# The first norm's four-element operations on GpSimd, its row sums in halves, and the last five batches scattered tile by tile

## What is computed

```python
xn = layernorm(x)                       # (x - m) / sqrt(v + 1e-5), no weights
q, k, v = relu(xn @ Wq + bq), relu(xn @ Wk + bk), relu(xn @ Wv + bv)
a = softmax(mask(q k^T / 4)) @ v        # 16 heads of 16; causal mask, mask of rows whose sum of xn is 0
attn = gamma * norm(a + xn) + beta      # second norm, eps 1e-8
moe = sum over the 2 best of 8 experts of w * (silu(xn w1) * (xn w3)) w2
out = x + attn + moe + shared expert of xn
```

## Time and profile before

| what | us |
|---|---|
| median of 3 runs | 2209.66 (2207.64 to 2210.34) |
| profiled execution, own time | 2199.74 |
| its span, first to last instruction | 2198.0 |
| attention phase, to the first instruction of the next | 1160.8 |
| expert phase | 1037.2 |

### The profile page before, as it was taken

One profiled execution on the slowest core, in us unless ns is written; L12 is line 12 of the kernel. 1 busy time (PEld: TensorE's weight loads), 2 busy tenths in 40 slices (PEclk: granted clock), 3 DMA queues, 4 the chain that ended last, 5 costly groups with the idle time before them and its releaser, 6 DMA issues. The chain is left out here.

```text
span 2198.0 us, 37336 instructions
## 1 busy us (share of the span) xinstructions
PE 1900.2 (86%) x13238; PEld 1375.1 (63%) x13238; DVE 1401.7 (64%) x2935; ACT 1082.8 (49%) x2048; POOL 1129.4 (51%) x935
## 2 busy tenths in 40 slices
PE   0368988888888888899676999999999999899998
PEld 0245544454554444555325888888888888788887
DVE  6577887788878888876513465656565543355556
ACT  0115555555455555555344666666666665333232
POOL 5444324544554454453423676867777764344443
PEclk9769999999999999999878999999999999999999
DMA  1653655666566666666345566666666654334443
GB/s 36 115 98 81 115 100 120 131 123 129 124 128 136 122 128 125 123 124 129 96 145 168 178 208 203 211 204 199 211 194 216 191 182 153 115 118 141 142 141 110
DMA packets 235391, 314.01 MB, mean 143 GB/s; under 512 B 18986, under 2 KB 200372, under 8 KB 229044
## 3 DMA queue, kind: packets, MB, share of 16 engines
q1 hardware_dynamic: 222964, 278.63, 51.0%
q0 software_dynamic: 12288, 33.57, 4.8%
HBM read 211.43 MB, written 100.70 MB: 142 GB/s over the span
## 5 line engine op out<-in xcount | busy, mean ns | idle before, releaser
L495 ACT ACTIVATE pT<-st_ps 128x512 f32<-128x512 f32 (+1 forms) x704 | 384.1, 559 | 477.0 <-PE st_ps L995 382.1
L1671 PE MATMUL gu<-xc,w_up_h 128*128 128x512 f32 x1760 | 553.1, 396 | 23.6 <-POOL w_up_l L1370 17.1
L719 DVE TENSOR_REDUCE mx<-s_ps 128x1 f32<-128x512 f32 (+3 forms) x704 | 436.2, 638 | 154.3 <-PE s_ps L974 123.4
L972 PE MATMUL s_ps<-k_aug,q_aug 97*128 97x512 bf16 (+3 forms) x1024 | 294.5, 320 | 138.8 <-DVE mx L719 124.0
L1671 PEld LDWEIGHTS gu<-xc,w_up_h 128*128 128x128 f32 x1760 | 326.3, 190 | 103.9 <-issue 18.0
L1671 PE MATMUL gu<-xc,w_up_l 128*128 128x512 f32 x880 | 345.1, 392 | 0.0
L1548 DVE TENSOR_TENSOR hf<-sil,gu 128x512 f32<-128x512 f32 x220 | 151.0, 686 | 258.8 <-ACT sil L1467 258.6
L1370 POOL TENSOR_TENSOR w_up_l<-w_raw,w_up_h 128x512 fp32r<-128x512 f32 x160 | 204.0, 1298 | 210.9 <-ACT w_up_h L1462 210.9
L993 PE MATMUL st_ps<-q_aug,k_aug 99*128 99x512 bf16 (+3 forms) x1024 | 286.5, 313 | 21.8 <-ACT pT L495 14.2
L972 PEld LDWEIGHTS s_ps<-k_aug,q_aug 97*128 97x128 bf16 x1024 | 101.9, 101 | 321.5 <-DVE mx L719 233.3
L411 POOL DMA_INDIRECT expert_rows<-xrow,slot x128 | 125.2, 978 | 314.5 <-DMA q_aug<-neg_scr 249.2
(11 more groups left out here) (207 smaller groups left out, 3418.1 us busy)
## 6 DMA issues: line engine op xcount, KB each, us to landing
w_raw<-in_L_ffn_w_dram SPq DMA_DIRECT2D x117, 512.0 KB, 6.0
part_scr<-parts SPq DMA_DIRECT2D x64, 384.0 KB, 9.3
q_aug<-part_scr SPq DMA_DIRECT2D x192, 128.0 KB
k_aug<-part_scr SPq DMA_DIRECT2D x192, 128.0 KB
xr<-expert_rows SPq DMA_DIRECT2D x39, 512.0 KB
expert_results<-yo SPq DMA_DIRECT2D x39, 512.0 KB, 3.3
x_sb<-in_L_attn_x_dram SPq DMA_DIRECT2D x16, 512.0 KB
layernorm_rows<-xn SPq DMA_DIRECT2D x16, 512.0 KB
```

What stands on the lines that cost most here:

```text
L495: fn(pT[:, j % 2, h:h + heads, 0:w], unit_view(st_ps[u % 2], heads, w), ACT.Exp).then_inc(exp_done, 1)
L719: vec.tensor_reduce(mx[:, q, h:h + heads], unit_view(s_ps[u % 2], heads, keys), AX_X, ALU.max).then_inc(s_max, 2)
L972: mm(v[:, n], q_aug[par][0:ROWS_S, h0 + n, P * q:P * (q + 1)], k_aug[par][0:ROWS_S, h0 + n, 0:keys], start=True, stop=False)
L1671: last = mm(gu[m % 2][:, a], w_up[wpar][x][:, a, c, P * m:P * (m + 1)], xc[par][:, y, c], start=k == 0, stop=k == 3 * NC - 1)
```

## The change

- **DVE keeps** the large operations of the first norm, the reciprocals and the bit cuts. **POOL takes** the folds, the multiplications and the rest of the root: 32 operations a batch beside its power. DVE's two-constant operations become two on POOL, with constants from a new tile `norm_consts`. Where DVE went on by itself, there are now semaphores both ways (`mean_part`, `mean_ready`, `var_part`, `s1_ready`, `r0_ready`, `d1_ready`, `r1_ready`, `root_ready`, `rd_ready`, `mask_part`, `mask_sum`).
- **Row sums** (mean, variance, mask) are made in halves of two tiles, in neighbouring units, so that a maximum comes between them. Some steps move by a unit: centre 3 to 4, product 24 to 25, bits 26 to 27, masks 41 and 42 to 40, 41 and 43.
- **Scatters**: body 14 does batches 11, 12 and 13, body 15 batches 14 and 15, each tile behind every third exponential; the wait for the negated maxima falls away in body 14. Fetches and bounds on SP move to fit.
- **Zeros**: `fill_ends` is done for four experts in body 14, once the table stands, ahead of `load_neg`, and for four in body 15. It no longer waits for the scatters.

```diff
-        AT_NORM = (1, 2, 3, 14, 15, 18, 20, 24, 26, 41, 42)
+        AT_MEAN, AT_CENTRE, AT_VAR = (1, 2), 4, (13, 14)
+        AT_R0, AT_R1, AT_RD, AT_QUOT, AT_BITS = 18, 20, 23, 25, 27
+        AT_MASKS = (40, 41, 43)
...
         def scattered_in(i):
-            if i == B - 1:
-                return list(range(B - GB, B))
-            return [i - 3] if 3 <= i < B - 1 else []
+            if i >= B - 2:
+                return {B - 2: [B - 5, B - 4, B - 3], B - 1: [B - 2, B - 1]}.get(i, [])
+            return [i - 3] if i >= 3 else []
...
-            def fill_ends():
+            def fill_ends(experts):
 
                 await_(sp, table_ready, 1)
-                for k in range(2):
-                    await_(sp, scattered[k], 16 * 2 * NT * (B // 2))
-                for e in range(E):
...
                     store_parts(i + 2, 1)
+                for b in scattered_in(i)[2:]:
+                    fetch(b)
+                if i == B - 2:
+                    fill_ends(range(E // 2))
                 if maxima:
                     load_neg(i + 1, 1 - par, 0)
                 for b in scattered_in(i + 1)[:2]:
                     fetch(b)
-                for b in scattered_in(i)[2:]:
-                    fetch(b)
                 if i == B - 1:
-                    fill_ends()
+                    fill_ends(range(E // 2, E))
 
             iterations(sp, body)
+            for k in range(2):
+                await_(sp, scattered[k], 16 * 2 * NT * (B // 2))
             await_(sp, filled, 16 * E)
...
+            small_begin, small_mark, small_op, small_end = chain(pool, chain_small, 28)
+
+            def fold4(a, b, final):
+                small_op(gp.tensor_tensor(tree2[:], a, b, ALU.add))
+                t2 = tree2[:].rearrange("p t (a b) -> p t a b", b=2)
+                small_op(gp.tensor_tensor(tree3[:], t2[:, :, :, 0], t2[:, :, :, 1], ALU.add))
+                return gp.tensor_tensor(final, tree3[:, :, 0], tree3[:, :, 1], ALU.add)
...
+            def small_mean(b):
+                small_begin(b)
+                await_(pool, mean_part, 2 * (b + 1))
+                small_op(fold16(s[SUM]))
+                await_(pool, a_ready, b)
+                gp.tensor_tensor(s[MEAN], s[SUM], inverse, ALU.mult).then_inc(mean_ready, 1)
+
+            def small_variance(b):
+                await_(pool, var_part, 2 * (b + 1))
+                small_op(fold4(lanes[:, :, 0:4], lanes[:, :, 4:8], s[SUM]))
+                small_op(gp.tensor_tensor(s[T1], s[SUM], inverse, ALU.mult))
+                small_op(gp.tensor_tensor(s[V1], s[T1], eps, ALU.add))
+                gp.tensor_tensor(s[S0], s[V1], half[:], ALU.pow).then_inc(s1_ready, 1)
+
+            def small_step(b):
+
+                await_(pool, r0_ready, b + 1)
+                small_op(gp.tensor_tensor(s[Q1], s[V1], s[R0], ALU.mult))
+                small_op(gp.tensor_tensor(s[T1], s[Q1], s[S0], ALU.add))
+                gp.tensor_tensor(s[D1], s[T1], half[:], ALU.mult).then_inc(d1_ready, 1)
+
+            def small_root(b):
+
+                await_(pool, r1_ready, b + 1)
+                small_mark(gp.tensor_tensor(s[SL], s[D1], s[SH], ALU.subtract))
...
+                small_op(gp.tensor_tensor(s[T1], s[T3], half[:], ALU.mult))
+                gp.tensor_tensor(s[ROOT], s[T1], s[D1], ALU.add).then_inc(root_ready, 1)
+
...
+            def small_parts(b):
+                await_(pool, root_ready, b + 1)
+                await_(pool, rd_ready, b + 1)
+                small_mark(gp.tensor_tensor(s[DL], s[ROOT], s[DH], ALU.subtract))
+                small_op(gp.tensor_tensor(s[NRD], s[RD], minus, ALU.mult))
+
+            def small_mask(b):
+                await_(pool, mask_part, 2 * (b + 1))
+                await_(pool, mk_ready, b)
+                fold16(s[MASK_SUM]).then_inc(mask_sum, 1)
+                small_end()
...
                 mine = scattered_in(i)
                 one = mine[0] if len(mine) == 1 else None
-                for b in mine if one is None else []:
-                    scatter(b, range(NT))
+                if norm:
+                    small_mean(i + 3)
+
+                if one is None:
+                    for n in range(len(mine) * NT):
+                        await_(pool, exp_done, NU * i + 2 + 3 * n)
+                        scatter(mine[n // NT], [n % NT])
 
...
-                    await_(pool, v1_ready, i + 4)
-                    gp.tensor_tensor(sm[:, 2], sm[:, 1], half[:], ALU.pow).then_inc(s1_ready, 1)
+                    small_variance(i + 3)
                 if project:
                     second(i + 2, 2)
+                if norm:
+                    small_step(i + 3)
                 if project:
                     second(i + 2, 3)
                     third(i + 2, 2)
+                if norm:
+                    small_root(i + 3)
                 if one is not None:
                     scatter(one, [2])
                 if project:
                     third(i + 2, 3)
                 if norm:
+                    small_parts(i + 3)
                     quotient(i + 3)
                 if one is not None:
                     scatter(one, [3])
+                if norm:
+                    small_mask(i + 3)
...
+            def row_sums(rows_, h):
+
+                t_ = slice(2 * h, 2 * h + 2)
+                return vec.tensor_reduce(lanes[:, t_], rows_[:, t_].rearrange("p t (k l) -> p t l k", l=16), AX_X,
+                                         ALU.add)
+
+            def ln_mean(b, h):
+                if h == 0:
+                    await_(dve, x_in, 16 * (b + 1))
+                    await_(dve, mask_sum, b)
+                row_sums(x_sb, h).then_inc(mean_part, 1)
 
             def ln_centre(b):
-                ln(vec.tensor_scalar(sm[:, MEAN], sm[:, SUM], 1.0 / C, None, ALU.mult))
+                await_(dve, mean_ready, b + 1)
+                await_(dve, normed, b)
                 for i in range(NT):
                     last = vec.tensor_scalar(ln_a[:, i], x_sb[:, i], sm[:, MEAN, i:i + 1], None, ALU.subtract)
                 last.then_inc(a_ready, 1)
 
-            def ln_var(b):
-
-                await_(dve, sq_done, b + 1)
-                ln(vec.tensor_reduce(lanes[:, :, 0:8], ln_t[:].rearrange("p t (w k) -> p t w k", k=C // 8), AX_X,
-                                     ALU.add))
-
-            def ln_var_fold(b):
-                fold4(lanes[:, :, 0:4], lanes[:, :, 4:8], sm[:, SUM], ln)
-                vec.tensor_scalar(sm[:, V1], sm[:, SUM], 1.0 / C, LN1_EPS, ALU.mult, ALU.add).then_inc(v1_ready, 1)
-
-            s = [sm[:, k] for k in range(20)]
-
-            def ln_root(b):
-
+            def ln_var(b, h):
+                if h == 0:
+                    await_(dve, sq_done, b + 1)
+                t_ = slice(2 * h, 2 * h + 2)
+                vec.tensor_reduce(lanes[:, t_, 0:8], ln_t[:, t_].rearrange("p t (w k) -> p t w k", k=C // 8), AX_X,
+                                  ALU.add).then_inc(var_part, 1)
+
+            def ln_r0(b):
                 await_(dve, s1_ready, b + 1)
-                ln(vec.reciprocal(s[R0], s[S0]))
-                ln(vec.tensor_tensor(s[Q1], s[V1], s[R0], ALU.mult))
-                ln(vec.tensor_tensor(s[T1], s[Q1], s[S0], ALU.add))
-                ln(vec.tensor_scalar(s[D1], s[T1], 0.5, None, ALU.mult))
-                ln_mark(vec.reciprocal(s[R1], s[D1]))
-
-                ln(vec.tensor_scalar(s[SH].bitcast(U32), s[D1].bitcast(U32), HIGH_BITS, None, ALU.bitwise_and))
-
-            def ln_root_end(b):
-                ln(vec.tensor_tensor(s[SL], s[D1], s[SH], ALU.subtract))
...
-                ln(vec.scalar_tensor_tensor(s[ROOT], s[T3], 0.5, s[D1], ALU.mult, ALU.add))
-                ln_mark(vec.reciprocal(s[RD], s[ROOT]))
-                ln(vec.tensor_scalar(s[DH].bitcast(U32), s[ROOT].bitcast(U32), HIGH_BITS, None, ALU.bitwise_and))
-                ln_mark(vec.tensor_tensor(s[DL], s[ROOT], s[DH], ALU.subtract))
-                ln(vec.tensor_scalar(s[NRD], s[RD], -1.0, None, ALU.mult))
+                vec.reciprocal(s[R0], s[S0]).then_inc(r0_ready, 1)
+
+            def ln_r1(b):
+                await_(dve, d1_ready, b + 1)
+                vec.reciprocal(s[R1], s[D1])
+                vec.tensor_scalar(s[SH].bitcast(U32), s[D1].bitcast(U32), HIGH_BITS, None, ALU.bitwise_and
+                                  ).then_inc(r1_ready, 1)
+
+            def ln_rd(b):
+                await_(dve, root_ready, b + 1)
+                vec.reciprocal(s[RD], s[ROOT])
+                vec.tensor_scalar(s[DH].bitcast(U32), s[ROOT].bitcast(U32), HIGH_BITS, None, ALU.bitwise_and
+                                  ).then_inc(rd_ready, 1)
 
             def ln_quotient(b):
+                ln_begin(b)
...
+                        if s in AT_MEAN:
+                            ln_mean(i + 3, AT_MEAN.index(s))
+                        if s == AT_CENTRE:
                             ln_centre(i + 3)
-                        if s == AT_NORM[3]:
```

(62 more changed lines are left out.)

72 lines of the change are left out of this document (31 added, 41 removed).

## The result

| what | before | after |
|---|---|---|
| median, us (least to most) | 2210.0 (2207.6 to 2210.4) | 2177.4 (2172.9 to 2179.7) |
| profiled execution, own time | 2199.7 | 2175.6 |
| first exponential | 160.2 | 163.1 |
| i = 0 to 12 | 818.7 | 812.0 |
| i = 13 | 57.0 | 59.9 |

The ratio is 0.9852, interval [0.9833, 0.9871]: 32.6 us faster, where 43 were forecast, and inside the range. The profiled executions differ by 24.2 only, since that of before was 10.3 under its median and that of after 1.8. The tail gave what was forecast; the iterations, from which 26 us were to come, gave 6.7.

A forecast was written before the change was run, and what follows sets the result against it. Bounds: row maxima that DVE's norm work makes late for PE, and late semaphores beside scatter bursts in the last two iterations. Sum -26 + 3 - 20 = -43 from 2209.7 gives 2166.7 us; range 2142 to 2200.

The forecast's parts named there:

- Prologue, +3: First batch's bare norm chain: 29 operations at 0.08 us more each, plus handoffs, 3 us longer; bounds +2 and +9.
- Steps on POOL, 0.28: Each chained 128x4 operation moved to POOL takes 0.28 us from start to start, against 0.20 on DVE.
- rival of slower steps: Slower root on POOL, mean step 0.38: 2195 us, chance 0.17; or POOL becomes the bound at 0.50: 2236, chance 0.08.
- Middle, 1.2 an iteration: Root's move to POOL brings the next maximum 1.4 us earlier, a little over PE's 1.1 slack; 1.2 us gained.
- Masks 0.8, mean 0: Per iteration: mask folds leaving DVE before the last maximum gain 0.8 us; mean's folds gain 0, bounds -0.3 and +0.3.
- Iterations, -26: Norm's edits save 2.0 us in each of 13 iterations; bounds 3.3 lost and 2.8 gained an iteration.
- What is queued behind the new waits: POOL's work behind R0 and R1 stores its last parts 1 us later, hidden by SP's loads of the other half.
- The third tile: Its scatter, queued on POOL behind R0 and R1 between third 2 and third 3, was to cost nothing.
- Tail, -20: Last two iterations: 20 paced tiles at 0.75 us, 15 in place of the bursts' 35.7; bounds -35 and +1.
- the pacing paces nothing: Rival: spaced scatters are still bursts, each tile costing its 1.8 us; 2188 us, chance 0.13.
- Zeros, 0: Moving half the zero stores ahead of `load_neg` in body 14 costs nothing; up to 5 us if cover is gone.
- Signs named beforehand: Iterations 61.0 us for 63.0, PE's maximum waits 1 to 2 less each, i = 14 about 57, i = 15 some 7 shorter.

The follow-up runs named there:

- e7: Changed kernel with two tiles scattered ahead of second 0, no wait for the negated maxima, and the root back on DVE: 2132.2 us, 0.9820 of before.
- e2: Kernel before with only the new scatters of the last five batches and the new place of the zeros: 2184.4 us, 0.9901 of before.
- e12: Changed kernel with three tiles scattered ahead of second 0 and no wait for the negated maxima: 2122.1 us, 0.9621 of before.
- e5: Kernel before with its first two tiles scattered ahead of second 0 and no wait for the negated maxima: 2160.6 us, 0.9959 of before.
- first set: Four runs on one chip: norm's edits alone, e2, and changed kernel without the gate's wait, with one or two tiles early; kernel before beside them 2205.6 us.
- e10: Changed kernel without the waits that pace the last 20 tiles, on the same chip as e9: 2200.2 us, 0.9966 of before.
- e9: Changed kernel itself, run once more without further edit: 2174.6 us, 0.9849 of before.
- second set: Four runs on one chip: e5, e6, e7 and the same edit as e12; kernel before beside them 2168.3 us.
- e6: Changed kernel without the pacing waits, the same edit as e10, run in the second set: 2149.9 us, 0.9910 of before.
- e11: Changed kernel with two tiles scattered ahead of second 0 and no wait for the negated maxima, beside e12: 2127.5 us, 0.9651 of before.

## Why the prediction was right, and where it was wrong

- **Prologue, +3**: 2.9. Right; its price of 0.08 us an operation is the 0.28 of POOL less the 0.20 of DVE, which the trace bears out.
- **Steps on POOL, 0.28**: right. Neither rival of slower steps came, and DVE waited for the mean 0.5 us at most and for the root not at all. The rule that the prediction took from the Trainium skill (GPSIMD Engine Reference, Engine selection) would have had 0.40: for elements this few the trace shows 0.28 beside DVE's 0.20, a factor of 1.4 and not 2.
- **Middle, 1.2 an iteration**: too small. e7 has 2.7 without scatters and 2.0 in the mean with them. The step that failed is "PE, busy for 715.3 of 818.7 us, has 1.1 us of slack in those 8.3 and not 3.3". Units 18 to 23 took 9.2 us in i = 1 before and 6.2 after. A mean over 13 iterations said nothing of those units, where PE had been waiting for DVE.
- **Masks 0.8, mean 0**: with the variance's fold, 1.8 together by e7; no run parts them. The stretch from the first exponential to that of unit 10 gives that much: 15.3 us before and 13.5 after in i = 1. The argument for the mean was that i = 13, with no norm, is no faster there. It was weak: i = 13 takes 15.2 us in that stretch in before but 12.4 in e2, which has the same norm.
- **Iterations, -26**: -6.7, which is -8.9 in i = 0 and 1, -1.6 in i = 2 and +3.8 in i = 3 to 12. The prediction had nothing for the scatters that stand in POOL's order between its handoffs to DVE. They cost 43.4 us (the gate's wait 20.5, the second tile 22.9) and 10.1 for the third, together 53.5. With all three moved (e12) iterations 0 to 12 take 757.0 us, 61.7 less than before. Some 6 of these the kernel before can have without the norm's edits (e5: 625.9 for 631.5 in i = 3 to 12), so the norm's edits are worth about 55, twice the forecast, and POOL's order takes nearly all of it. Under "What is queued behind the new waits" the prediction looked only at work behind the waits that it added, and it read POOL's timeline from 688.01 on the earlier trace rows; the row with 18.55 us of idle time before the scatter, 9 us further up in the same view, plays no part in it. Nor was it asked, for each handoff that a faster DVE would reach earlier, what the other side was then waiting for.
- **The third tile**, whose place was to cost nothing ("so the last parts are stored 1 us later", which the loads hide): the tile and third 3 behind it now fall beside DVE's product, 2.60 us for 1.13.
- **i = 13, 57.0**, counted as unchanged: 59.9 in after, and between 54.3 and 61.3 in the other runs of the first set. It has the same gate: units 0 to 9 take 11.6 us for 15.2, but units 10 to 17 19.3 for 13.0, and DVE waits 5.7 us for second 0.
- **Tail, -20**: -14.1 - 8.7 = -22.8, by the mechanism given, late semaphores beside bursts, and a feedback that stops POOL: e10 against e9 and the 15 waits of POOL. That the pacing paces nothing, 0.13, fell. The price comes out near 0.75 us a tile: 35.7 - 22.8 leaves 12.9 for 20 tiles, 0.65 each. One wait of 3.7 us without a releaser is left on ACT. All this holds in this condition alone: in that of the second set there is no loss to win back.
- **Zeros, 0**: right in this condition, 10 us in the other.
- **Signs named beforehand**: iterations of 61.0 were to be seen and are 62.5 (812.0 / 13); i = 14 57 and is 56.0; i = 15 7 shorter and is 8.7; xn by unit 40, and it is ready at 714.54, just before the sum that wants it at 714.83. The sign that fails is the first, and with it "PE's wait on maxima down by 1 to 2 us each": 86.5 us became 78.7, 0.6 each. The list of what would be wrong held no wait of POOL's.
- **The sum**: the total of the profile's -43 became -24.2. That the median fell by 32.6 and so came near the forecast owes 8.4 us to how far each profiled execution stood from its median, not to the reasoning. Nor was the total near through its terms. A gain twice as large as forecast (about 55 for 26) and a loss that was not in the sum (53.5) nearly cancelled, and the time fell into the range by luck for the larger of its two terms; the tail's term was right by its mechanism.

## What to carry to other kernels

Before giving work from a busy engine to an idle one, list every wait in the second engine's order at its old time of the iteration, and ask which of them the first engine will now reach sooner; a gate that costs nothing today may be just behind the bound. Iterations that lack one ingredient (here i = 0 and 1, without scatters) show what the rest of a change is worth by itself, though not what it is worth with that ingredient (the root 2.7 us and 2.0). Work on a helper engine that nothing waits for, here scatters of 2.5 us a tile, belongs where the helper is idle anyway, not between its handoffs.

## What the runs showed of the hardware

- **Late semaphores beside scatters and gathers.** ACT waited up to 13.57 us with no releaser (e10) while GpSimd issued indirect DMAs back to back, which cost 25.6 us for the last 40 scatters in e10 against e9. In the second set such bursts cost nothing (e5, e6), and none of its four kernels has such a wait anywhere. A time of this kernel means little without the kernel before beside it: the two conditions differ by 1.7%.
- **DVE beside POOL.** The product took 2.60 us beside a scatter and third 3 and 1.13 without, the rounding 1.36 beside second 1 and 0.43 without. e12's DVE is busy 12.5 us less than e11's by one move of two scatters. In i = 8 of after it looks like the operation behind the scatter: one product instruction ran beside the scatter in 0.34 us, and the next, of 1.81, ended 0.16 us after third 3; the rounding ended 0.29 us after second 1 (676.89 + 1.36 against 675.70 + 2.26). No run moves third 3 alone. The Trainium skill (SBUF — State Buffer, SBUF: two separate sides) says that a VectorE operation in a two-port mode and a GpSimd operation lock each other out for a whole instruction. The trace agrees in that both slow instructions of DVE end just after POOL's; it shows neither the lock nor the mode that DVE's instructions ran in.
- **Small operations on GpSimd** with 4 elements a partition cost 0.20 us, 0.28 from start to start when chained, for additions, subtractions and multiplications alike; a power 1.04.
